# Scores of turns 1 and 15 in two halves of four graphs, with the T1 tile between them

## What is computed

```python
q, k, v = split_heads(x @ Wq.T + bq), split_heads(x @ Wk.T + bk), split_heads(x @ Wv.T + bv)
scores = einsum('bhsd,bhtd->bhst', q, k) * SCALE
attn = softmax(where(mask, scores, -1e9), axis=-1)
x = layernorm(x + einsum('bhst,bhtd->bhsd', attn, v) @ Wo.T + bo)
Wh = einsum('bni,hoi->bhno', h, W) + bW
e = einsum('bhno,hop->bhnp', Wh, attn1)
A_mat = tanh(where(adj, einsum('bhnp,bhmp->bhnm', e, Wh), 0))
ha = cat(relu(A_mat @ Wh)) @ A_w.T ;  hf = h @ fc_w.T
c = sigmoid(hf @ g1_w.T + ha @ g2_w.T + gbias)
x = layernorm(x + hf * c + ha * (1 - c))
```

## Time and profile before

| | |
|---|---|
| median of three runs | 1092.28 us (1091.84 to 1094.07) |
| the profiled execution | 1093.23 us |
| its span in the trace | 1091.4 us |
| PE busy | 1079.9 us, 99% |
| weight loads of PE busy | 907.3 us, 83% |
| DVE busy | 706.7 us, 65% |
| ACT busy | 542.1 us, 50% |
| POOL busy | 290.2 us, 27% |

### The profile page before, as it was taken

One profiled execution on the slowest core, in us unless ns is written; L12 is line 12 of the kernel. 1 busy time (PEld: TensorE's weight loads), 2 busy tenths in 40 slices (PEclk: granted clock), 3 DMA queues, 4 the chain that ended last, 5 costly groups with the idle time before them and its releaser, 6 DMA issues. The chain is left out here.

```text
span 1091.4 us, 25406 instructions
## 1 busy us (share of the span) xinstructions
PE 1079.9 (99%) x10102; PEld 907.3 (83%) x10102; DVE 706.7 (65%) x1318; ACT 542.1 (50%) x980; POOL 290.2 (27%) x277
## 2 busy tenths in 40 slices
PE   9999999999999999999999999999999999999997
PEld 6888788888888888788888888888888888888887
DVE  7785766666676575765756666575765757666544
ACT  5663553625446373563735446363562735546352
POOL 1542231232322223322232322223322222322200
PEclk9999999999999999999999999999999999999999
DMA  7000100100010000100100010000100001010000
GB/s 263 2 24 20 41 24 21 41 20 19 22 40 22 20 19 22 40 22 20 40 13 28 22 40 22 20 19 22 40 22 20 22 18 40 22 35 9 1 20 20
DMA packets 26861, 32.60 MB, mean 30 GB/s; under 512 B 4432, under 2 KB 23376, under 8 KB 26448
## 3 DMA queue, kind: packets, MB, share of 16 engines
q1 hardware_dynamic: 26400, 31.93, 8.8%
q10 hardware_dynamic: 432, 0.26, 0.1%
HBM read 23.80 MB, written 8.39 MB: 29 GB/s over the span
## 5 line engine op out<-in xcount | busy, mean ns | idle before, releaser
L953 ACT ACTIVATE cat_hi<-bank 128x512 fp32r<-128x512 f32 x128 | 76.6, 598 | 127.1 <-PE bank L396 127.1
L916 ACT ACTIVATE T<-bank 128x512 f32<-128x512 f32 x128 | 75.0, 604 | 86.7 <-PE bank L396 86.7
L1086 DVE SCALAR_TENSOR_TENSOR cat_lo<-bank,cat_hi 128x512 fp32r<-128x512 f32 x128 | 86.6, 686 | 39.1 <-ACT cat_hi L953 36.9
L391 PE MATMUL bank<-hT_hi,g_lo 128*128 128x512 f32 x256 | 102.6, 401 | 0.0
L385 PE MATMUL bank<-cat_hi,aw_hi 128*128 128x512 f32 (+1 forms) x272 | 102.4, 377 | 0.0
L384 PE MATMUL bank<-cat_hi,aw_lo 128*128 128x512 f32 (+1 forms) x272 | 102.4, 377 | 0.0
L383 PE MATMUL bank<-cat_lo,aw_hi 128*128 128x512 f32 (+1 forms) x272 | 102.4, 377 | 0.0
L392 PE MATMUL bank<-U_hi,wt_hi 128*128 128x512 f32 x256 | 99.8, 390 | 0.0
L391 PE MATMUL bank<-U_hi,wt_lo 128*128 128x512 f32 x256 | 99.8, 390 | 0.0
L392 PE MATMUL bank<-hT_hi,g_hi 128*128 128x512 f32 x256 | 99.8, 390 | 0.0
L1452 POOL TENSOR_TENSOR probs<-probs,den 128x512 f32<-128x512 f32 x64 | 67.5, 1057 | 119.6 <-DVE den L1177 119.4
(11 more groups left out here) (198 smaller groups left out, 2750.2 us busy)
## 6 DMA issues: line engine op xcount, KB each, us to landing
y<-in_x SPq DMA_DIRECT2D x16, 512.0 KB, 3.5
out<-res SPq DMA_DIRECT2D x15, 512.0 KB, 3.0
x_raw<-in_xT SPq DMA_DIRECT2D x14, 512.0 KB, 3.3
W_nat<-in_Wn SPq DMA_DIRECT2D x1, 1028.0 KB, 7.7
attn_nat<-in_attn SPq DMA_DIRECT2D x1, 1024.0 KB, 9.6
adjS_u<-in_adjS SPq DMA_DIRECT2D x32, 32.0 KB, 2.8
raw_A<-in_AwT SPq DMA_DIRECT2D x1, 1024.0 KB, 8.8
x_second<-in_xT SPq DMA_DIRECT2D x1, 512.0 KB, 10.3
```

Of the source, the lines that this page charges most:

```text
L391: pe.matmul(out, wsel(w[1]), dsel(d[0]), start=first and n == 0, stop=False)
L916: take(act.activation(T[:, n % DC, n // DC, :], bank[:], ACT.Copy), "B", f"T{n}", g)
L953: act.activation(cat_hi[:, n, :], bank[:], ACT.Relu).then_inc(cat_hi_ready, 1)
L1086: return dve.scalar_tensor_tensor(out=out, in0=bank, scalar=bias, in1=hi.bitcast(F32), op0=op, op1=ALU.subtract)
```

## The change

In turns 1 and 15, and in these alone, PE makes the scores of graphs 0 to 3 after T0, then T1, then the scores of graphs 4 to 7, then T2. The waits and claims of the scores are done with the first half. The loop's turns, turn 0, and the lists of all other engines stay as they are.

```diff
-            def scores(g):
-                for n in ("q0", "q1", "k0", "k1"):
-                    await_taken(pe, "A", n, g)
-
-                for j in range(JB):
-                    claim(pe, "A", f"score{j}", g)
-                for b in range(NG):
+            def scores(g, graphs):
+                if 0 in graphs:
+                    for n in ("q0", "q1", "k0", "k1"):
+                        await_taken(pe, "A", n, g)
+                    for j in range(JB):
+                        claim(pe, "A", f"score{j}", g)
+
+                for b in graphs:
...
-                    scores(0)
+                    scores(0, range(NG))
...
                 for n in range(KC):
                     T_tile(B, n)
+
                     if A is not None and n == 0:
-                        scores(A)
+                        scores(A, range(NG // 2 if isinstance(A, int) else NG))
+                    if isinstance(A, int) and n == 1:
+                        scores(A, range(NG // 2, NG))
```

## The result

The changed kernel takes 1096.23 us (median of 8 runs, 1095.0 to 1096.58) against 1092.89 (8 runs, 1091.72 to 1094.13) before: a ratio of 1.0023 with a 95% interval of 1.0012 to 1.0034. It is slower, by 2.5 us going by the ratio and 3.3 by the medians; the profiled spans are 1094.4 and 1091.4 us, 3.0 apart. Forecast were 3.1 us more, and 1095.4 us with a range of 1093.4 to 1096.6.

A forecast was written before the change was run, and what follows sets the result against it. PE was taken to bound the kernel, busy 1079.9 of 1091.4 us. Turn 1's 1.61 and turn 15's 1.51 sum to 3.12 us, giving 1095.4 us on the median 1092.28, with a range of 1093.4 to 1096.6.

The forecast's parts named there:

- The bound: PE is busy 1079.9 of 1091.4 us and has no wait in turns 1 and 15; any new wait is lost time.
- The divided block: On PE in turns 1 and 15, one more block of scores costs 0.21 us per turn, bounds 0 and 0.42.
- Turn 15: Scores 1.57 us later delay ACT's first exponential and four result activations behind it; T4 waits, starting 1.51 us later.
- e0: First exponential on ACT, after DVE's shift 0; in turn 15 forecast to start at about 979.24 instead of 977.67.
- The release time: From ACT's release of a bank to PE's waiting matmul: 0.36 us, read in the last turn.
- Turn 1: POOL's hT goes ahead of DVE's first subtraction, which ends 2.37 us later; adj_scores waits for T7's copy, 1.61 us later.
- the small wait at T6: In turn 1, PE's T6 waits 0.26 us for T2's bank, 60.08 against 59.82.
- e2: Third exponential on ACT; in turn 1 forecast at 63.47 instead of 61.87, making the copies of T6 and T7 late.
- DVE wins the race: In turn 1 DVE's subtraction goes before hT, so the turn costs 0.21 us; total 1.7 us, 1094.0; chance 0.14.
- The stall at the loop's entry absorbs it: Turn 2's 1.1 us issue stall is gone when PE comes later, leaving 2.0 us, 1094.3; chance 0.08.
- Only the transitions: In turns 1 and 15 no bank is late, so 2 x 0.21 = 0.4 us remain, 1092.7; chance 0.08.
- A faster kernel: Needs a PE wait that goes away; at most turn 2's 1.1 us stall could, giving 1091.6; chance 0.04.

The follow-up runs named there:

- with ACT reordered: Changed kernel with halves in all turns, result activations ahead of the first exponential, copies of T4 to T7 ahead of third and fourth: 1098.7 us, ratio 1.0047.
- the first two experiments: Changed kernel with the halves in turn 1 alone: 1094.48 us, ratio 1.0012; in turn 15 alone: 1093.6 us, ratio 1.0007.
- both causes are removed: Changed kernel with POOL's h_lo, hT and gate weight's low part ahead of group 1's mask, and result activations ahead of the first exponential in turn 15: 1093.71 us, ratio 1.0005.

## Why the prediction held

**The bound.** PE had no wait in either turn, so every new one is lost time. It held: what PE had lost up to `adj_scores` (1.61 and 1.50 us) it had lost over the whole turn (1.60 and 1.53).

**The divided block** was mis-sized: 0.21 us forecast from the entry and the exit of one block, with 0.42 as the upper bound; 0.43 measured in turn 1 (0.37 to 0.44 over the kernels), 0.43 per loop turn with ACT reordered. What I left out is inside the block. Two halves take 0.85 us each from start to the next tile's start, 1.70 against the whole block's 1.52: a fixed 0.18 per block, so that "the scores only divide" was wrong. T1 between them takes 1.58 where a tile takes 1.36, the 0.21 of the forecast to 0.01. The Trainium skill's page TensorEngine Tiling (Array Packing), section "Key Properties", says that a change of tiling mode drains the TensorE; it gives no price. The rows give one for leaving and entering a block as a whole; no run shows how much of it is the drain.

**Turn 15.** The mechanism is as forecast, e0 late and four result activations behind it. Two terms were off, against each other. The scores come 1.75 us later, not 1.57, because of the 0.18 above. The release time was taken as 0.36 from a place with two more waits; it is 0.05 at T4, with one wait. So T4 comes 1.37 us later and not 1.51, and the margin before was 0.4 us, not 0.06. After the wait T4 itself takes 1.50 where a tile takes 1.36, the cold start which I had as a bound (0.15). At `adj_scores` 1.50 against 1.51 forecast is thus right in size partly by luck.

**Turn 1.** Forecast 1.61, measured 1.61 to `adj_scores` and 1.60 over the turn. hT went first as forecast. The subtraction ends 0.55 after hT, and not the 0.80 that a pause and a full 0.69 us would give. The copy of T7 ends 15.33 us after T0 (15.36 forecast) and PE goes on 0.39 later (0.36 forecast), so here the mechanism and the sizes both fit. Only the small wait at T6 (0.26) was wrong: PE was itself 0.43 late by then, and T2's copy ended at 59.81, 0.38 before T6. It changed nothing, since e2 and the copies of T6 and T7 set the end.

**The rivals.** "DVE wins the race" fell for the change, where the subtraction starts 0.38 us after hT. But the race is a near one: with scores 0.39 us earlier (whole, after T1) hT was first by 4 ns in the traced execution, and by the times probably not in most others. "The stall at the loop's entry absorbs it" fell: the stall (0.84 and 1.10 in the two profiled executions) is there or not with the same list before it, and 1.10 was also seen with PE late (the changed kernel with its waits reordered). It always comes at one place, behind the 117th of 128 matmuls, as the prediction held against this rival; what it is stays open. So a changed stall was no good sign of being wrong: it did change, by 0.26, and said nothing of the forecast. Its absence in the first two experiments is why their spans missed. "Only the transitions" fell for the change, and is what is left when both causes are removed. A faster kernel had nothing to come from.

**The signs.** The two new waits came where they were named. The one at `adj_scores` is 1.13 in the view (1.1 to 1.3 forecast), the one at T4 0.77 in the view and 0.95 by starts (1.1 to 1.3). The subtraction took 2.57 us (2.8) and ended 0.55 after hT. A half block took 0.85 us and not 0.76.

**The size.** 3.1 us forecast, 3.0 by the distances and spans, 2.5 by the ratio with 1.3 to 3.7 as its interval. The median of 1096.23 lies 0.8 over the forecast 1095.4; 0.6 of it is that before's own median is 1092.89 over 8 runs and not 1092.28.

## What to carry to other kernels

When an engine is full, the price of moving work on it is read from the others' lists: look at what stands behind the first instruction that will be late, and not only at who waits for it. Here four result activations, ready long before, stood behind an exponential; with them ahead of it the same edit cost 0.4 us in turn 15 in place of 1.5. And a small shift of the scores (1.4 us, whole after T1) can cost more than itself (2.3 us at the end of DVE's subtraction) where it lets another engine's long operation go first. Where a race is near, one trace shows one outcome only: compare it with all the times.

## What the runs showed of the hardware

- DVE's subtraction with both inputs in SBUF and POOL's operations on SBUF exclude each other here, in the order of their recorded starts, and a subtraction that is held ends 0.54 to 0.55 us after POOL's operation. POOL's next operation starts about 0.05 us before the running one ends. A subtraction that started 1.4 us before that end (the kernel before) went ahead of it; one that started 0.05 us before it, 4 ns behind POOL's next, was held through that one too.
- One more block of K = 32 matmuls between 128x128 ones costs 0.43 us in the changed kernel: 0.18 in the block and 0.25 at its borders. Over all kernels it is 0.37 to 0.44.
- PE resumes 0.05 us after the end of the instruction that releases it where one wait is left, 0.15 where the last of several waits is the late one, and 0.36 to 0.39 where two waits stand behind that. The tile after such a wait (T4) takes 1.50 us where others take 1.36.
- Executions of one kernel differ by stalls of PE that no semaphore explains. At the loop's entry there were 1.10, 0.84 or 0 us, always behind the 117th matmul of the same block of scores. In turn 0 there was one of 2.37 at the attention with halves in all turns, and one of 2.09 in the execution of the reordered waits:

```profile
PE bank L550 <- issue: 2.1, 1, 2.1
```

  These are as large as the effect under study. Distances within turns 1 and 15 are free of them, and the timed medians are not. Their cause stays open.
